# A Mamba block's front on one core: transposes of x moved on TensorE, VectorE's third part, delta steps and moments re-ordered

## Time and profile before

| | us |
|---|---|
| median of 3 runs | 2267.18 (2264.71 to 2272.36) |
| the profiled execution | 2264.66 |
| its span, first to last instruction | 2262.8 |
| start of the first scan | 193.16 |
| start of the scans without a pause | 201.56 |

### The profile page before, as it was taken

One profiled execution on the slowest core, in us unless ns is written; L12 is line 12 of the kernel. 1 busy time (PEld: TensorE's weight loads), 2 busy tenths in 40 slices (PEclk: granted clock), 3 DMA queues, 4 the chain that ended last, 5 costly groups with the idle time before them and its releaser, 6 DMA issues. The chain is left out here.

```text
span 2262.8 us, 50361 instructions
## 1 busy us (share of the span) xinstructions
PE 2139.4 (95%) x16960; PEld 1260.6 (56%) x16960; DVE 1841.2 (81%) x2779; ACT 1598.0 (71%) x2070; POOL 944.1 (42%) x452
## 2 busy tenths in 40 slices
PE   7887999999999999999999997999999999999997
PEld 3342333333333333333333335899999999999986
DVE  5768999999999999999999997565565566556665
ACT  4677988888888888888888884555455455544543
POOL 3225343434444443434343443544444444444442
PEclk9895999999999999999999999999999999999999
DMA  5887222222221212122221225100100010000000
GB/s 166 249 242 190 44 45 44 46 41 45 42 46 39 46 39 46 39 49 42 46 45 41 47 47 149 38 0 0 38 1 0 0 38 1 0 1 1 10 10 18
DMA packets 354957, 114.93 MB, mean 51 GB/s; under 512 B 283000, under 2 KB 345600, under 8 KB 354624
## 3 DMA queue, kind: packets, MB, share of 16 engines
q1 hardware_dynamic: 350416, 110.92, 20.0%
q10 hardware_dynamic: 4464, 3.02, 0.4%
HBM read 67.98 MB, written 45.88 MB: 50 GB/s over the span
## 5 line engine op out<-in xcount | busy, mean ns | idle before, releaser
L1518 DVE TENSOR_TENSOR_SCAN arena<-behind 128x1040 f32<-128x1040 f32 x512 | 1157.1, 2310 | 6.9 <-ACT behind L961 4.3
L1062 ACT ACTIVATE arena<-PS,arena 128x512 f32<-128x512 f32 x512 | 343.1, 689 | 395.7 <-PE PS L1294 395.4
L951 ACT ACTIVATE behind<-PS 128x1024 f32<-128x1024 f32 x512 | 527.3, 1030 | 133.7 <-DVE arena L1518 101.3
L1197 PE MATMUL PS<-arena 128*32 128x128 f32 x8192 | 565.9, 406 | 0.0
L961 ACT ACTIVATE behind<-PS 128x1024 f32<-128x1024 f32 x512 | 539.2, 1053 | 7.4 <-PE PS L1180 3.8
L1306 PEld LDWEIGHTS PS<-arena 128*128 128x128 f32 x4096 | 476.3, 193 | 7.9
L1306 PE MATMUL PS<-arena 128*128 128x128 f32 x4096 | 476.6, 276 | 0.0
L771 POOL COPY behind<-carry 128x64 f32<-128x64 f32 x128 | 209.3, 1635 | 517.2 <-DVE arena L1518 382.1
L1294 PE MATMUL PS<-parts_xh,parts_w 128*128 128x512 f32 x1536 | 383.6, 401 | 14.4 <-ACT arena L1062 13.6
L1197 PEld LDWEIGHTS PS<-arena 128*32 128x32 f32 x8192 | 234.6, 119 | 287.7 <-issue 210.5
L1180 PE MATMUL PS<-arena 96*128 96x512 bf16 x1024 | 314.4, 389 | 53.0 <-ACT behind L961 38.7
(11 more groups left out here) (131 smaller groups left out, 1413.1 us busy)
## 6 DMA issues: line engine op xcount, KB each, us to landing
dl_d<-arena SPq DMA_DIRECT2D x48, 256.0 KB, 3.0
du_d<-arena SPq DMA_DIRECT2D x48, 256.0 KB, 3.3
arena<-dl_d SPq DMA_DIRECT2D x512, 24.0 KB
arena<-b_d SPq DMA_DIRECT2D x64, 192.0 KB
arena<-du_d SPq DMA_DIRECT2D x512, 24.0 KB
b_d<-arena SPq DMA_DIRECT2D x48, 128.0 KB, 2.8
u_d<-behind SPq DMA_DIRECT2D x8, 512.0 KB, 4.1
sz_d<-arena SPq DMA_DIRECT2D x8, 512.0 KB, 4.8
```

The costliest lines, as they stand in the source:

```text
L951: nc.scalar.activation(seg(dA[:, half])[:, :, 1:], PS[:, 0:2, :].rearrange("p j (i t) -> p (j i) t", t=TC), ACT.Exp).then_inc(exp_done, 1)
L1062: nc.scalar.activation(hT[:, e % 2, c], PS[:, HIDDEN[(GT * e + c) % 3], :], ACT.Gelu, bias=bias1[:, lp, e * GT + c:e * GT + c + 1]).then_i ...
L1197: last = nc.tensor.matmul(PS[32 * j:32 * j + 32, 4 + kk, 0:DB], cd[:, pair, j, 32 * i:32 * i + 32], seg(hb[kk])[:, :, 1 + 16 * j + i], sta ...
L1518: nc.vector.tensor_tensor_scan(hb[kk][:, q * QD * SEG:(q + 1) * QD * SEG], dA[:, q % 2], dB[:, G_, lo:lo + QD * SEG], 0.0, ALU.mult, ALU.a ...
```

## The change

PE: `turn_x(k+2)` stands right behind the convolution of item k+1, ahead of L1145 and of `gate_of(k+1)`. DVE: B's split of item k stands behind the third part of item k-1 and behind the delta steps of item k, which move from the head of item k+1 (and, for item 7, from behind the loop). The moments and the norm of x are done for item k+3 at the end of item k, and not for item k+2 at its head. Nothing is added to or taken from the work: the same instructions and DMAs are issued.

```diff
@@ PE, loop over k
                     for h in range(HALVES):
                         inner(k + 1, h)
+                if k < ITEMS - 2:
+                    turn_x(k + 2)
...
                 last.then_inc(a_btp, 1)
                 if k < LAST:
                     gate_of(k + 1)
-                if k < ITEMS - 2:
-                    turn_x(k + 2)
@@ DVE, loop over k
                 bb = k % 2
-                if k < ITEMS - 2:
-                    input_moments(k + 2)
-                if k > 0:
-                    steps(k - 1)
-                if k < ITEMS - 2:
-                    input_norm(k + 2)
-                if k > 0:
+                if k == 0:
+                    input_moments(2)
+                    input_norm(2)
+                else:
                     remainder(k - 1)
...
+                if k > 0:
+                    dve.wait_ge(a_p1, k)
+                    nc.vector.tensor_tensor(part[1 - bb][2], rest[1 - bb], part[1 - bb][1], ALU.subtract
+                                            ).then_inc(a_p2, 1)
+                steps(k)
+
                 if k > 1:
                     dve.wait_ge(a_rows[bb], ROW_STORES * (k // 2))
                     dve.wait_ge(a_blo, k - 1)
...
                                         ALU.subtract).then_inc(a_brest, 1)
-                if k > 0:
-                    dve.wait_ge(a_p1, k)
-                    nc.vector.tensor_tensor(part[1 - bb][2], rest[1 - bb], part[1 - bb][1], ALU.subtract
-                                            ).then_inc(a_p2, 1)
-            steps(LAST)
+                if k + 3 < ITEMS:
+                    input_moments(k + 3)
+                    input_norm(k + 3)
```

## The result

The changed kernel takes **2246.35 us** (median of 6 runs, 2244.75 to 2249.00) beside 2265.78 (2264.71 to 2272.36) for the kernel before, 6 runs: a ratio of 0.9911 [0.9898, 0.9924], 19.4 us faster. The forecast was 2243.0 in a range of 2234 to 2253. The profiled execution took 2246.93 us, its span is 2245.1, 17.7 less than before.

What follows compares the result with a forecast made beforehand. One ring through convolution, transposes, SiLU and L1127 paced the front; after the change, transfers would end it. First scan at 169.0 for 193.16, 24.2 us earlier, against the median 2267.18 gives 2243.0 us; range 2234 to 2253.

Steps and rivals of the forecast that it cites:

- Gap and clock: Ahead of L1127 on PE: the gap shrinks from 3.54 to 0.4 us and L1127 takes 1.94 us for 3.33.
- Cast 0.40, root 1.01, DVE's wait 1.19: POOL's cast 0.40 us and square root 1.01 us, DVE waiting 1.2 us at the norm; DVE's ring 16.8 us.
- Transfers end the front: Stores ahead of the product loads, not engines, end the front: products' data at 159 us, first scan at 169.0.
- Rival A: Front: transfers run above 306 GB/s and are not the bound, engines start scanning at 160; 2234 us; chance 10%.
- the time of the transfers: From B's first store at 38.9 us: 111.8 us of stores plus 3 dry, through at 153.7, landed at 155.
- the allowance of 3 us: SP's queue in items 1 and 2 still waits for B's low part: 3 us dry, none later.
- Late next: Item 7's row stores are down at 192 us, when the second block's first scan is due: just covered.
- Behind the scans: Whatever brings the first scans forward moves all that follows by as much; the gain is 24.2 us.
- Rival B: Front: PE's clock falls at 0.4 us gaps, POOL is slow, or transfers lose a tenth; gain 17, 2250 us; 18%.
- C: Ln waits behind norm and remainder, so the 3.5 us gap ahead of L1127 returns; 2262 to 2267 us; 5%.
- D: SP's B stores wait for B's low part, DMA engines dry 5 us an item; slower, 2277 us; 4%.

Runs made afterwards that it cites:

- the run with the third part behind: The changed kernel with the third part left behind B's split, only the steps ahead of it: 2244.45 us, ratio 0.9907 to the kernel before.
- the early split: The changed kernel with B's split of items 0 and 1 ahead of the third part and the steps: 2252.59 us, ratio 0.9938 to the kernel before.
- the deferred stores in the kernel before: The kernel before with 24 part stores moved from the front to the block stage as DRAM copies: 2266.24 us, ratio 0.9992.
- the deferred stores and the late norm added: The changed kernel with B's split early in items 0 and 1, 24 stores deferred and the norm behind the remainder: 2244.54 us, ratio 0.9914.

## Why the prediction was right, and where a term was off

- **Gap and clock**: right here, but the clock was in part luck. 0.18 to 0.74 us stand where 0.4 was forecast, and L1127 takes 1.94 in every item. The Trainium skill (TensorE: Matmul & The Clock Gate, "A second HAM failure mode") says that PE's frequent short stops between groups of matmuls make the clock swing; by that L1127 could have stayed near 3.3. In this execution it didn't, nor behind gaps of 1.3 to 1.6 us in the run with the third part behind; but behind 1.23 us in item 1 of the early split the next groups were slow, and behind 0.68 us in item 0 of four executions (last section). The prediction says that no row has such a short gap. The trace of before has one in item 0: L1136 takes 1.98 us, full speed, behind 0.68.
- **Cast 0.40, root 1.01, DVE's wait 1.19**: the forecast's values. The items are 16.4 to 16.6 us apart at 38.35, 54.82, 71.18, 87.67, 104.31 and 120.81 (16.8 forecast), item 7 at 136.23 (137 to 139). One reading was wrong: the remainder doesn't get its input later than the norm ends. ACT's L899 ends at 75.36, the norm at 77.69, and with the norm behind the remainder the items came 0.4 us closer.
- **Transfers end the front**: right, shown by two kernels. With the same order of the engines and 24 fewer stores ahead of the scans the first scan gains 8 to 9 us, and in the kernel before the same edit gives nothing. Rival A falls. Its rates too: B's stores run near 213 GB/s as in the earlier trace rows, and the mix at a full share gives 290, below the 306 that I took for the likeliest, let alone the 400 of A.
- **The mis-sized term** is the time of the transfers: silu(z) landed at 159.2, not 155, the products' data at 162.6, not 159, the first scan at 171.4, not 169.0. The stretch from B's first store to that landing is 120.2 us by the windows. The forecast had 114 of work (its 1.4 for the store under way are 1.3 by its own figures), over 1.02, plus 3 dry, plus 1.3 to land, 116.1. Measured are 0.97 x 120.23 = 116.6 of work, 2.6 more (the same product for the kernel before, with 0.83 of 138.7 us, is 115.1, which is the same within the rounding: a share is given to 0.01, and 0.005 of 120 us is 0.6). A full stretch (58.62 to 153.67) reads 0.99 rather than 1.02, 3.4 us: the 1.04 of the earlier trace rows came from a stretch of part stores alone and doesn't hold for the mix of an item. Dry are some 2.4 us, nearly all in item 1 (0.6 less), and the landing lies in the work already (1.3 less). 2.6 + 3.4 - 0.6 - 1.3 = 4.1, the lateness of silu(z). Two small ones give 1.8 back: data 3.4 behind silu(z) for 4, and 8.8 us from the data to the first scan for 10. In sum 2.4 late, the 21.7 us for 24.2.
- **The wait in item 1** was in the allowance of 3 us, but for another reason than I gave: less the moved split than the norm at 4.21 us beside POOL's clear. So that the allowance held was luck. The trace of before had this very pair, DVE's norm and POOL's clear, and it was overlooked:

```profile
42.17 2.75 DVE L1368 TENSOR_SCALAR arena<-arena 128x128 f32<-128x128 f32 x4
...
40.75 3.51 POOL L742 MEMSET arena<- 128x4096 f32 x1 [0.15 <-POOL arena L688]
```

- **Late next**: right. Item 7's row stores are down at 195.6, not 192, and the second block's first scan waits 0.24 us for them.
- **Behind the scans** the forecast kept everything as it was. The stretch from the last scan to the end varies from 886.1 to 890.5 us over all profiled executions with no bond to the edits (886.1 for PE's part alone, 890.5 for the deferred stores in the kernel before; 890.1 and 887.3 for the changed kernel itself). In the profiled execution after, PE's clock reads 0.93 from 1569 to 1619, before 1.00 from 1590 to 1640. So its span gained 17.7 us where its scans gained 21.7; the medians gave 19.4, and 21.0 when it was run again. What sets that clock was not tested.
- **Rival B**: no tenth more work, no ring of 19 us; its mechanisms fell for this kernel, though the time, 2246, stands between it and the forecast. **C** needed a ring of 20.5 us, and the items are 16.6 us apart at most. **D** had its place right, SyncE behind B's low part, but it was 2.0 us in one item, not 5 in six. The side on which the change could really have lost was not among the rivals: had DVE's steps stayed in their place, PE's part would have cost 21 us.

## What to carry to other kernels

When a wait of the bounding ring is taken away, name what that wait covered: here the delta's steps, 4.79 us behind it, and one half of the change lost 21 us where both together won 19. Once the engines are faster than the transfers, take the DMA time from a stretch with the same mix of transfers, and count bytes next. A pace a few tenths of a us under the new bound is free, so test which part of a reordering is needed at all.

## What the hardware did that was not expected

- A stop of PE is mostly paid by what comes behind it. Behind 4.79 us (PE's part alone) the next three groups took 14.5 us for 10.2. Behind 3.54 to 3.69 us L1127 took from 2.90 to 3.69, but once, in item 1 with DVE's part alone, 1.94 behind 3.68.
- How short a stop is free can't be told from its length here. Behind 1.30 to 1.59 us L1127 took 1.94 four times, with the granted clock at 1.00. Behind 1.23 us ahead of L1110 in item 1 of the early split, L1136 took 2.82 for 1.98 and the convolution 9.6 for 7.14; behind 1.23 us in the same place, with the deferred stores and the late norm added, both were at full speed.
- The clock can also fall where PE hardly stops. In item 0 of the kernel before with deferred stores (lines stand 9 further down: L1145 is L1136, L1099 is L1090):

```profile
25.18 2.37 PE L1145 MATMUL PS<-behind 8*128 8x512 f32 x4 [0.68 <-ACT behind L932]
27.47 10.10 PE L1099 MATMUL PS<-arena,behind 128*128 128x512 f32 x16
```

  The convolution took 10.10 us for 7.14 behind a gap of 0.68, with a granted clock of 0.70 in the mean. That of item 0 took 8.5 to 10.2 in four of the thirteen profiled executions, of both orders of work, and 7.14 in the others, with the same gap. It moves a single execution by up to 3 us, and was not explained.
- DVE's norm took 4.21 us beside POOL's clear of 3.51 us, and 1.11 without, though a clear reads nothing. It was the same in all seven executions that had the two start together; in the three where the norm started 1.4 us behind the clear, the kernel before among them, it took 2.75. In the kernels after and before it ended 0.66 us behind the clear's end (44.70 and 44.04; 44.92 and 44.26), as if most of it had waited for the clear. Two other operations of DVE show the same: a cast of item 0 (L1417) took 2.64 us beside a clear and 0.23 without in both kernels, and 1 + exp of item 7 took 4.12 us for 0.69 in the kernel before with deferred stores, both through by 0.1 to 0.6 us behind the clear's end. Only the norm was moved away as a test.
- Stores for which SyncE waited less lay closer together without disturbing each other: 116.6 us of DMA work for 115.1, the same within the rounding.
